# The depthwise convolution of one sample moved from TensorE's products to taps on VectorE, inside the attention of the sample before it

## The chip, the cores and the metric

The kernel runs on one core of one Trainium2 chip. The metric is the time of one execution on the device, in microseconds (us). It covers the whole program: sixteen samples, from the first load to the last store.

## The reference, cut to what matters

```python
x = x + L0(gn(x))      # whitening: power iterations on a covariance over all samples, once
x = x + L1(gn(x))      # deformable convolution, depthwise 3x3 in front of it
x = x + L2(gn(x))      # window attention: 64 windows of 49 tokens + 1, 16 heads of 32
x = x + L3(gn(x))      # masked 3x3 convolution, 128 -> 128 channels

# in L1; x is [16, 128, 56, 56], f32 throughout
xproj = x @ in_w + in_b
x1 = depthwise_conv3x3(x, dw_w) + dw_b          # one 3x3 filter for each channel
mu, var = x1.mean(-1), ((x1 - mu) ** 2).mean(-1)   # over the 128 channels of a pixel
x1 = gelu((x1 - mu) / sqrt(var + 1e-5) * ln_g + ln_b)
offset, mask = x1 @ off_w + off_b, softmax(x1 @ mask_w + mask_b)
out = bilinear_samples(xproj, offset, mask) @ out_w + out_b
```

## The kernel before, in words

Channels lie on the 128 partitions, and a sample is 3136 pixels on the free axis, in seven chunks of 8 rows (448 pixels). Every engine's program is written out by hand in its own order, and semaphores are all that ties them together. After a start that works out the whitening (some 490 us) one loop runs over the samples. Its body has two stages.

The first stage, `windows(i, n)`, is the attention of sample i. It runs in 32 **slots** (`for s in range(PAIRS)`), each for two windows and all heads. Between the attention's operations each slot carries a piece of the next sample's (n = i + 1) L1. The second stage, `sample_tiles(n, i)`, does the sampling of n and the rest of i, in 35 steps.

In slot s the attention's operations are, engine by engine and in this order:
- TensorE: `scores(s + 1)` (L747), `turn_exps(s)` (transposes, L758), `weigh(s - 1)` (L774), `values(s + 1)` (L733), two `queries_keys` (L725; slots 0 to 26 only). Ahead of `turn_exps(s)` stands `taken(s - 1, n)`, a wait until the banks that the last slot's piece of L1 used have been read, and a wait until both `queries_keys` of the last slot have been copied out. Ahead of the `queries_keys` stands a wait for VectorE's `turned(s)`.
- VectorE: `shift(s + 1)`, a maximum (L1738) and a subtraction (L1740) on the scores; `turned(s)`, a copy of half the transposed numbers (L1747); `normalise(s - 1)` (L1754, L1756); a copy of the odd `queries_keys` (L1732).
- ScalarE: a copy of the other half (L1140), the exponentials (L1134), copies of values and of the even `queries_keys` (L1127, L1122).

The piece of L1 has a fixed place in a slot: `before_first` at the slot's head and `before_last` at its end on VectorE and ScalarE, and `before5` and `before4` (named after the PSUM bank) behind the `queries_keys` on TensorE. Which piece a slot carries is set by constants, `GN0_AT, XP_AT, DW_AT, VAR_AT, BC_AT, OFF_AT = 2, 4, 8, 16, 18, 24`:
- slots 4 to 7 hold the projection of the image, two chunks a slot: ScalarE writes tiles (L1091), TensorE projects them (L671), and VectorE adds the bias into `img` one slot later (L1697);
- slots 8 to 14 hold the depthwise convolution, one chunk a slot, as nine products (L663) of the padded input `vp` with `dwc`, nine 128 x 128 matrices that hold the filter's diagonal times the centring matrix (identity minus 1/128), so that the sum comes out less its mean over the channels. ScalarE reads each chunk twice in the slot after it (L1071 to `x1c`, L1072 its square to `y1`);
- slot 16 holds the variance (L713); in slot 17 VectorE takes the reciprocal of seven rows of standard deviations (L1718);
- slots 18 to 21 spread these rows over the channels (L677), and VectorE multiplies them in (L1705);
- at the end of slot 22 ScalarE does the Gelu; slots 24 and 25 hold the projection to offsets and mask; slots 27 and 28 hold the mask's sum and product, and slots 29 to 31 the three `by_row` (L1640, L1646) for the sampling's first chunk.

`Chain.step` on VectorE and ScalarE makes the engine wait until the operation just issued is done. SyncE's queue issues `windows_out(i, s)` (L444) in each slot. In slot 9 it also issues `image_columns` (16 copies, L401 and L403), and in slot 11 `image_rows` (L408, L409).

For sample 0 the same pieces of L1 run ahead of the loop with no attention between them. The last sample's attention (the 16th block) carries no next sample.

Of the kernel before, what the change touches and what calls it, by code (L numbers as in the profile page):

```python
# [45 lines left out]
POW_D, POW_P = 9, 9  # L46
DVE_A, DVE_COV, DVE_POW = 20, 12, 22
ACT_MAIN = 14
DVE_PRE, DVE_MAIN, DVE_BLK, DVE_END = 6, 112, 69, 46

GN0_AT, XP_AT, DW_AT, VAR_AT, BC_AT, OFF_AT = 2, 4, 8, 16, 18, 24
TWO = (CHUNKS + 1) // 2
# [46 lines left out]
def build(nc, a):  # L99
    with ExitStack() as ctx:  # L100
# [13 lines left out]
        dwc = sb("dwc", [C, P9, C])  # L114
# [77 lines left out]
        mask16, mean128, centre = cv(C), cv(C), cv(C)  # L192
# [106 lines left out]
        cp_col, cp_img = sig("columns_copied", 2 * TY * 16), sig("rows_copied", 2 * 16)  # L299
        dw_p, dw_s = sig("dw_psum", CHUNKS), sig("dw_sbuf", CHUNKS)  # L300
# [38 lines left out]
        block = ctx.enter_context(nc.Block())  # L339
        WEIGHTS = 18 * 16  # L340
# [213 lines left out]
        def _(pe):  # L554
# [82 lines left out]
            def taken(s, n):  # L637
# [5 lines left out]
                elif DW_AT <= s < DW_AT + CHUNKS:  # L643
                    pe.wait_ge(dw_s.sem, dw_s.at(n, s - DW_AT + 1))
# [41 lines left out]

            def before4(s, n):

                if XP_AT <= s < XP_AT + TWO:
                    project_in(n, 2 * (s - XP_AT) + 1, 4)  # L690
                elif BC_AT <= s < BC_AT + TWO:
                    spread_rows(n, 2 * (s - BC_AT) + 1, 4)
                else:
                    project_bias(0, 4)
                    project_tile(n, 0, 2 * (s - OFF_AT), 4).then_inc(of_p.sem, 1)

            def before5(s, n):
# [6 lines left out]
                elif DW_AT <= s < DW_AT + CHUNKS:  # L704
# [311 lines left out]
            for s in range(PAIRS):  # L1016
                if in_bank5(s):
                    taken(s - 1, 0)
# [15 lines left out]
        def _(act):  # L1034
# [29 lines left out]
            def before_first(s, n):  # L1064
# [18 lines left out]
            def before_last(s, n):  # L1083

                if XP_AT - 1 <= s < XP_AT - 1 + TWO:
                    if s == XP_AT - 1:
                        act.wait_ge(gn_ab[0].sem, gn_ab[0].at(n))
                    for k in range(2 * (s - (XP_AT - 1)), min(2 * (s - (XP_AT - 1)) + 2, TR)):
# [4 lines left out]
                elif XP_AT - 1 + TWO <= s < XP_AT - 1 + 2 * TWO:  # L1093
                    for k in range(2 * (s - (XP_AT - 1 + TWO)), min(2 * (s - (XP_AT - 1 + TWO)) + 2, CHUNKS)):
                        rows = slice(k * ROWS, (k + 1) * ROWS)
                        nc.scalar.activation(vp_in[:, rows, :], xa[:, k * CH:(k + 1) * CH].rearrange("c (h w) -> c h w", w=W),
# [895 lines left out]
```

## Time and profile before

| | us |
|---|---|
| time, median of 3 runs | 11480.75 (11474.91 to 11494.1) |
| time of the profiled execution | 11494.43 |
| its span, first to last instruction | 11492.6 |
| TensorE matmul busy | 9424.9 (82%) |
| TensorE weight load busy | 5065.9 (44%) |
| VectorE busy | 6877.1 (60%) |
| ScalarE busy | 3657.9 (32%) |

The mean granted clock of TensorE was 0.869 of full speed. The busy shares are means over stages that differ, so the rows below are read stage by stage. **M(s)** stands for the start of VectorE's maximum (L1738) number s of a stage, s from 0 to 31. M(s) to M(s + 1) is one slot's length, with TensorE's piece of L1 from slot s - 1 in it. The stage looked at starts with M(0) at 5689.93 us. In it M(4) = 5716.14, M(9) = 5753.10, M(16) = 5844.29, M(17) = 5850.52, M(19) = 5870.58, M(23) = 5909.55 and M(31) = 5979.59, and the second stage's first `multiply` starts at 5993.97.

### The profile page before, as it was taken

The page shows a single profiled execution, that of the slowest core. Times are in us where ns is not written, and L with a number is a line of the kernel's source. Part 1 is how long each engine was busy: PE and PEld are TensorE (multiplying, and loading weights), DVE is VectorE, ACT ScalarE, POOL GpSimd, SP SyncE. Part 2 cuts the span into 40 slices and gives each one's busy share as a digit, 9 for nine tenths or more (in the row PEclk, how much of TensorE's full clock was granted, in tenths as well). Part 3 has the DMA queues.
Part 4 walks back from the last instruction along what each step waited for, and adds up shares of the span by engine and source line. Part 5 has one row for each costly group of instructions (what it writes and reads, how often), then busy time and mean ns, then how long its engine had stood idle before and what let it go on. Part 6 is the DMA issues. An engine that isn't in the chain of part 4 may idle for free.

```text
span 11492.6 us, 291312 instructions
## 1 busy us (share of the span) xinstructions
PE 9424.9 (82%) x125822; PEld 5065.9 (44%) x125822; DVE 6877.1 (60%) x8513; ACT 3657.9 (32%) x5874; POOL 216.2 (2%) x254
## 2 busy tenths in 40 slices
PE   5578888897888889798888878888797888888887
PEld 5324444353444435344443534435354443534444
DVE  2365756647466564846657475665747566574663
ACT  0023333242333324333232433324233332423322
POOL 0000000000000000000000000000000000000000
PEclk7668898898989888898888989889898988989888
DMA  4001101111110111111011111101011011111101
GB/s 99 17 0 33 41 25 36 30 33 35 36 42 19 39 33 31 37 35 40 22 39 29 36 38 33 35 26 41 27 37 39 26 35 30 35 34 36 41 17 51
DMA packets 230329, 391.97 MB, mean 34 GB/s; under 512 B 25200, under 2 KB 166480, under 8 KB 221776
## 3 DMA queue, kind: packets, MB, share of 16 engines
q1 hardware_dynamic: 229008, 372.66, 11.7%
q8 instruction: 1036, 16.97, 0.6%
q14 instruction: 285, 2.33, 0.1%
HBM read 192.47 MB, written 130.55 MB: 28 GB/s over the span
## 4 chain that ended last, share of the span: by engine, by line
PE 62%; DVE 20%; issue 10%; ACT 6%; DMA 1%; POOL 0%; DVEq 0%; SPq 0%; ACTq 0%; POOLq 0%
PE ps L663 13%; PE ps L857 9%; PE ps L725 8%; PE ps L733 4%; DVE arena L1663 4%; PE ps L758 4%; PE ps L774 4%; DVE arena L1640 3%; PE ps L956 3%; DVE arena L1646 3%; PE ps L946 3%; PE ps L747 2%; PE ps L685 2%; DVE arena L1629 1%; PE ps L682 1%
## 5 line engine op out<-in xcount | busy, mean ns | idle before, releaser
L857 PE MATMUL ps<-arena,ident 64*64 64x512 f32 x5600 | 1972.1, 738 | 923.4 <-DVE arena L1663 890.2
L859 PE MATMUL ps<-arena,ident 48*64 48x512 f32 x5600 | 1978.9, 740 | 0.0
L1663 DVE TENSOR_TENSOR arena<-arena 112x2560 f32<-112x2560 f32 x560 | 1573.5, 2817 | 2.4 <-PE ps L859 2.4
L857 PEld LDWEIGHTS ps<-arena,ident 64*64 64x64 f32 x5600 | 529.7, 158 | 2051.8 <-issue 2041.4
L1738 DVE TENSOR_REDUCE arena<-ps 128x16 f32<-128x800 f32 x512 | 505.8, 988 | 929.0 <-PE ps L747 921.2
L725 PE MATMUL ps<-arena,wqk 128*128 128x400 f32 x2048 | 964.9, 595 | 101.9 <-DVE arena L1747 54.4
L1732 DVE COPY arena<-ps 128x400 f32<-128x400 f32 x512 | 294.6, 575 | 1119.0 <-PE ps L725 1119.0
L663 PE MATMUL ps<-vp,convw 128*128 128x448 f32 x2016 | 819.5, 552 | 23.6 <-ACT vp L1269 23.6
L758 PE MATMUL ps<-ident,arena 128*128 128x128 f32 x4096 | 621.1, 300 | 213.2 <-ACT arena L1072 66.7
L663 PE MATMUL ps<-vp,dwc 128*128 128x448 f32 x2016 | 786.6, 543 | 8.3 <-ACT arena L1072 7.5
L1646 DVE TENSOR_TENSOR arena<-arena 112x576 f32<-112x576 f32 x1008 | 764.0, 758 | 34.9
L774 PE MATMUL ps<-arena 64*64 64x33 f32 x32768 | 681.8, 235 | 92.1 <-issue 53.1
L733 PE MATMUL ps<-wv,arena 128*64 128x256 f32 x4096 | 636.7, 437 | 103.2 <-ACT arena L1140 92.5
L774 PEld LDWEIGHTS ps<-arena 64*64 64x64 f32 x32768 | 613.7, 151 | 198.2 <-issue 198.0
L1640 DVE TENSOR_TENSOR arena<-arena 112x1728 f32<-112x1728 f32 x336 | 656.0, 1953 | 3.4
L725 PEld LDWEIGHTS ps<-arena,wqk 128*128 128x128 f32 x2048 | 355.5, 210 | 608.9 <-issue 238.1
L758 PEld LDWEIGHTS ps<-ident,arena 128*128 128x128 f32 x4096 | 492.5, 153 | 261.1 <-issue 126.4
L1134 ACT ACTIVATE arena<-arena 128x800 f32<-128x800 f32 x512 | 447.8, 875 | 446.1 <-DVE arena L1740 445.1
L663 PEld LDWEIGHTS ps<-vp,convw 128*128 128x128 f32 x2016 | 371.2, 192 | 480.1 <-issue 456.4
L747 PEld LDWEIGHTS ps<-arena 32*64 32x64 f32 x32768 | 403.6, 134 | 366.8 <-issue 358.3
L663 PEld LDWEIGHTS ps<-vp,dwc 128*128 128x128 f32 x2016 | 371.8, 189 | 397.2 <-issue 335.1
L1140 ACT ACTIVATE arena<-ps 128x512 f32<-128x512 f32 x512 | 305.7, 597 | 742.2 <-PE ps L758 742.1
(285 smaller groups left out, 12500.5 us busy)
## 6 DMA issues: line engine op xcount, KB each, us to landing
windows_out<-arena SPq DMA_DIRECT2D x1024, 100.0 KB
arena<-windows_out SPq DMA_DIRECT2D x224, 256.0 KB, 3.9
arena<-windows_out SPq DMA_DIRECT2D x224, 192.0 KB, 3.4
arena<-in_wqk SPq DMA_DIRECT2D x16, 2048.0 KB, 8.8
arena<-in_x_t SPq DMA_DIRECT2D x16, 1568.0 KB, 11.5
arena<-in_x SPq DMA_DIRECT2D x16, 1568.0 KB, 6.7
arena<-arena SPq DMA_DIRECT2D x32, 784.0 KB
out_x<-xb SPq DMA_DIRECT2D x112, 224.0 KB, 1.9
```

The lines of the kernel that those rows point to most:

```text
L663: mm = nc.tensor.matmul(ps[:, bank, 0:CH], weights[:, tap, :], vp[:, ROWS * k + dy:ROWS * k + dy + ROWS, dx:dx + W], start=(tap == 0), sto ...
L725: nc.tensor.matmul(ps[:, 5 - m % 2, 0:NWY * NTOK], wqk[:, m * C:(m + 1) * C], xwb[b % 2][:, :, 0:NTOK], start=True, stop=True).then_inc(qk ...
L733: mm = nc.tensor.matmul(ps[hh * SLOT:(hh + 1) * SLOT, 4, wi * 256:(wi + 1) * 256], xwb[b % 2][:, 2 * pr + wi, :], wv[:, hh * 256:(hh + 1) ...
L747: mm = nc.tensor.matmul(ps[wi * SLOT:(wi + 1) * SLOT, r, place * NTOK:(place + 1) * NTOK], qk[b % 2][32 * r:32 * r + 32, m, w:w + SLOT], q ...
L758: mm = nc.tensor.transpose(ps[:, 4 + q, k * C:(k + 1) * C], e_sb[u][:, 8 * q + 2 * k:8 * q + 2 * k + 2, :], ident)
L774: mm = nc.tensor.matmul(ps[wi * SLOT:(wi + 1) * SLOT, 6 + hh, (kk * 4 + r) * VD:(kk * 4 + r + 1) * VD], et[u][hh * SLOT:(hh + 1) * SLOT, a ...
L857: nc.tensor.matmul(ps[half, 3, :], ident[0:SLOT, 0:SLOT], prod[0:SLOT, ring(c, dy), dx, :], start=(s < 2), stop=(s >= TAPS - 2), skip_grou ...
L859: mm = nc.tensor.matmul(ps[half, 4, :], ident[SLOT:PT, SLOT:], prod[SLOT:PT, ring(c, dy), dx, :], start=(s < 2), stop=(s >= TAPS - 2), ski ...
L1640: ownm.step(V.tensor_tensor(tt[0:PT, :].rearrange("p (a n) -> p a n", a=3), hat[0:PT, :, 0, :], hat[0:PT, bb, 1:2, :].to_broadcast([PT, 3, ...
L1646: ins = V.tensor_tensor(k5, k5, tt[0:PT, aa * HN:(aa + 1) * HN].rearrange("p (x y n) -> p x y n", x=3, y=3), ALU.add)
L1663: V.tensor_tensor(prod[0:PT, ring(c, dy), :, :].rearrange("p k (n e) -> p k n e", e=CG), taps.to_broadcast([PT, SHIFTS, N64, CG]), for_tap ...
L1738: ownb.step(V.tensor_reduce(mxs[u].rearrange("p (r m) -> p r m", r=4), sv, AX.X, ALU.max))
```

## The change

The nine products with `dwc` go. VectorE now sums the nine taps itself: `depthwise(n, j)` multiplies a shifted view of `vp` by one filter value for each channel and adds it to `x1c`, two chunks (896 pixels) at once, 36 operations a sample (four blocks of nine; the last block has one chunk, 448 pixels). Three of them stand in each of the slots 5 to 16: behind `shift`, behind `turned`, and behind the copy of the `queries_keys`. TensorE then does the centring alone, one product of `centre` with each chunk (slots 12, 13, 15 and 17, up to two a slot in banks 5 and 4), which ScalarE reads as before. The other pieces move in the table: the padded input is written first (slots 3 to 6), the image's projection goes to slots 8 to 11, the variance from slot 16 to 18, the spreading from 18 to 20 and the offsets from 24 to 25. The third `by_row` of the first chunk moves from slot 31 into the second stage, behind its first `multiply`. `image_columns` and `image_rows` follow the projection, from slots 9 and 11 to 13 and 15. In the lines below, `pe` is TensorE, `dve` VectorE, `act` ScalarE.

```diff
+GN0_AT, V1_AT, XP_AT, VAR_AT, BC_AT, OFF_AT = 2, 3, 8, 18, 20, 25
+DW_BLOCKS = (CHUNKS + 1) // 2
+DW_SLOTS = (5, 5, 5) + (6, 6, 6) + (7, 7, 7) + (8, 8, 8) + (9, 9, 9) + (10, 10, 10) + (11, 11, 11) + (12, 12, 12) + (13, 13, 13) + (14, 14, 14) + (15, 15, 15) + (16, 16, 16)
+CT_AT = {12: (0, 1), 13: (2, 3), 15: (4, 5), 17: (6,)}
-GN0_AT, XP_AT, DW_AT, VAR_AT, BC_AT, OFF_AT = 2, 4, 8, 16, 18, 24
...
+            def centred(n, k, bank):
+                pe.wait_ge(dw_d.sem, dw_d.at(n, k // 2 + 1))
+                nc.tensor.matmul(ps[:, bank, 0:CH], centre, x1c[:, k * CH:(k + 1) * CH], start=True, stop=True
+                                 ).then_inc(dw_p.sem, 1)
...
-                elif DW_AT <= s < DW_AT + CHUNKS:
-                    k = s - DW_AT
-                    pe.wait_ge(v1_in.sem, v1_in.at(n, min(k + 2, CHUNKS)))
-                    for dy in range(3):
-                        mm = conv_row(k, 5, dwc, dy)
-                    mm.then_inc(dw_p.sem, 1)
+                elif s in CT_AT:
+                    centred(n, CT_AT[s][0], 5)
...
+            def depthwise(n, j):
+
+                b, tap = j // P9, j % P9
+                ks = dw_block(b)
+                dy, dx = tap // 3, tap % 3
+                acc = x1c[:, ks[0] * CH:(ks[-1] + 1) * CH].rearrange("c (h w) -> c h w", w=W)
+                around = vp[:, ROWS * ks[0] + dy:ROWS * (ks[-1] + 1) + dy, dx:dx + W]
+                if tap == 0:
+                    dve.wait_ge(v1_in.sem, v1_in.at(n, min(ks[-1] + 2, CHUNKS)))
+                    ownp.step(V.tensor_scalar(acc, around, dww[:, tap:tap + 1], None, ALU.mult))
+                    return
+                ins = V.scalar_tensor_tensor(acc, around, dww[:, tap:tap + 1], acc, ALU.mult, ALU.add)
+                if tap == P9 - 1:
+                    ins.then_inc(dw_d.sem, 1)
+                else:
+                    ownp.step(ins)
...
-                elif OFF_AT + 5 <= s < OFF_AT + 8:
+                elif OFF_AT + 5 <= s < OFF_AT + 7:
                     by_row(n, 0, s - (OFF_AT + 5))
...
-                        if c and dy == 0:
+                        if dy == 0:
                             by_row(n, c, 2)
```

VectorE in the loop's first stage, before, one slot of the depthwise stretch:

```order
L1738 TENSOR_REDUCE arena<-ps 128x16
L96 REGISTER_ALU
L1740 TENSOR_TENSOR arena<-ps,arena 128x800
L1747 COPY arena<-ps 128x512
L1754 RECIPROCAL arena<-ps 128x16
L96 REGISTER_ALU
L1756 TENSOR_TENSOR arena<-ps,arena 128x512
L1729 REGISTER_ALU
L1732 COPY arena<-ps 128x400
```

The same engine now, slot 10 (L1739 is a tap, L1713 the image's bias that was L1697, L105 the wait of `Chain.step`):

```order
L1776 TENSOR_REDUCE arena<-ps 128x16
L105 REGISTER_ALU
L1778 TENSOR_TENSOR arena<-ps,arena 128x800
L1739 SCALAR_TENSOR_TENSOR arena<-vp,cols,arena 128x896
L105 REGISTER_ALU
L1785 COPY arena<-ps 128x512
L1739 SCALAR_TENSOR_TENSOR arena<-vp,cols,arena 128x896
L1792 RECIPROCAL arena<-ps 128x16
L1794 TENSOR_TENSOR arena<-ps,arena 128x512
L1770 COPY arena<-ps 128x400
L1739 SCALAR_TENSOR_TENSOR arena<-vp,cols,arena 128x896
L1713 TENSOR_TENSOR arena<-ps,inb_row 112x512 x2
```

Three taps have come in between the six operations, and in slots 9 to 12 two bias additions stand with them.

TensorE before, from one slot's depthwise products to the next slot's:

```order
L663 MATMUL ps<-vp,dwc 128x448 x9
L747 MATMUL ps<-arena 64x50 x32
L758 MATMUL ps<-ident,arena 128x128 x8
L774 MATMUL ps<-arena 64x33 x32
L733 MATMUL ps<-wv,arena 64x256 x4
L725 MATMUL ps<-arena,wqk 128x400 x2
```

TensorE now, slot 12 to slot 13 (L704 is the centring; L765, L776, L792, L751 and L743 are the five attention groups):

```order
L704 MATMUL ps<-arena,centre 128x448 x2
L765 MATMUL ps<-arena 64x50 x32
L776 MATMUL ps<-ident,arena 128x128 x8
L792 MATMUL ps<-arena 64x33 x32
L751 MATMUL ps<-wv,arena 64x256 x4
L743 MATMUL ps<-arena,wqk 128x400 x2
```

Nine products a slot in seven slots have become two, two, two and one product in four slots.

## Rows read from the trace of the kernel before

**Rows 1.** The page: the chain that ended last, by engine.

```profile
PE 62%; DVE 20%; issue 10%; ACT 6%; DMA 1%; POOL 0%; DVEq 0%; SPq 0%; ACTq 0%; POOLq 0%
```

**Rows 2.** Stretches: length; PE, PEld, DVE, ACT, POOL busy (x); granted clock; DMA.

```profile
5716.14:5753.10 36.96, 34.62 (x796) 24.89 (x796) 25.12 (x40) 24.25 (x34) 0.00 (x0) 1.00 0.10 31
5753.10:5844.29 91.19, 87.23 (x1162) 49.31 (x1162) 28.66 (x43) 30.72 (x51) 0.00 (x0) 1.00 0.22 52
5850.52:5870.58 20.06, 19.22 (x388) 10.79 (x390) 10.80 (x13) 8.72 (x12) 0.00 (x0) 1.00 0.08 23
5870.58:5909.55 38.97, 36.68 (x532) 21.50 (x528) 20.67 (x33) 10.42 (x17) 0.00 (x0) 0.69 0.08 23
5909.55:5979.59 70.04, 55.86 (x1264) 36.40 (x1266) 40.60 (x57) 37.20 (x55) 2.87 (x2) 0.90 0.09 26
...
11120.16:11125.72 5.56, 5.56 (x149) 3.72 (x150) 4.01 (x6) 2.58 (x4) 0.00 (x0) 1.00 0.13 39
5880.15:5890.90 10.75, 10.72 (x152) 6.56 (x152) 5.35 (x8) 2.58 (x4) 0.00 (x0) 0.64 0.07 21
5971.84:5979.59 7.75, 6.61 (x215) 5.24 (x215) 7.49 (x10) 2.33 (x4) 1.43 (x1) 0.92 0.12 35
```

**Rows 3.** TensorE in time order, one slot with depthwise products: start, length, line.

```profile
5769.39 1.71 PE L725 MATMUL ps<-arena,wqk 128*128 128x400 f32 x4
5770.94 7.02 PE L663 MATMUL ps<-vp,dwc 128*128 128x448 f32 x18
5777.89 0.89 PE L747 MATMUL ps<-arena 32*64 32x50 f32 x64
```

**Rows 4.** VectorE in time order, the same slot; in brackets idle time and releaser.

```profile
5765.72 0.99 DVE L1738 TENSOR_REDUCE arena<-ps 128x16 f32<-128x800 f32 x1 [7.10 <-PE ps L747]
5766.75 0.99 DVE L1740 TENSOR_TENSOR arena<-ps,arena 128x800 f32<-128x800 f32 x1
5767.66 0.68 DVE L1747 COPY arena<-ps 128x512 f32<-128x512 f32 x1
5768.52 0.26 DVE L1754 RECIPROCAL arena<-ps 128x16 f32<-128x16 f32 x1 [0.18 <-PE ps L774]
5768.90 0.69 DVE L1756 TENSOR_TENSOR arena<-ps,arena 128x512 f32<-128x512 f32 x1
5771.14 0.57 DVE L1732 COPY arena<-ps 128x400 f32<-128x400 f32 x1 [1.55 <-PE ps L725]
5778.82 0.99 DVE L1738 TENSOR_REDUCE arena<-ps 128x16 f32<-128x800 f32 x1 [7.11 <-PE ps L747]
```

**Rows 5.** VectorE by line and shape: count, busy us, mean ns, idle before.

```profile
L1697 DVE TENSOR_TENSOR arena<-ps,inb_row 112x512 f32<-112x512 f32 x112 | 77.5, 692 | 39.9 <-PE ps L671 39.9
L1882 DVE SCALAR_TENSOR_TENSOR xb<-ps,cols,xb 128x448 f32<-128x448 f32 x112 | 76.5, 683 | 621.6 <-PE ps L663 621.6
L1877 DVE SCALAR_TENSOR_TENSOR arena<-arena,cols,vp 128x3136 f32<-128x3136 f32 x16 | 55.7, 3480 | 0.0
L1420 DVE TENSOR_SCALAR arena<-arena 128x256 f32<-128x256 f32 x16 | 5.7, 355 | 0.6
```

**Rows 6.** TensorE in time order at the lower clock, inside 5880.15:5890.90.

```profile
5885.71 2.65 PE L725 MATMUL ps<-arena,wqk 128*128 128x400 f32 x4
```

**Rows 7.** SyncE's queue: `image_columns`, first and last of 16 issues.

```profile
5783.42 0.99 SPq L401 DMA_DIRECT2D arena<-arena  x1
...
5797.25 0.83 SPq L403 DMA_DIRECT2D arena<-arena  x1
```

**Rows 8.** VectorE in time order, the second stage's head.

```profile
5993.97 2.82 DVE L1663 TENSOR_TENSOR arena<-arena 112x2560 f32<-112x2560 f32 x1
5999.17 0.46 DVE L1606 TENSOR_REDUCE softmax_max<-ps 112x32 f32<-112x288 f32 x1 [2.38 <-PE ps L685]
```

**Rows 9.** Two source lines: min/median/max ns, first and last start.

```profile
L663 PE MATMUL ps<-vp,dwc x2016: 537/538/643, 526.6 to 10583.9; 128*128 128x448 f32 x184
L713 PE MATMUL ps<-arena,varsel x224: 539/539/543, 584.6 to 10601.0; 128*7 128x448 f32 x112
```

More of the change, by code:

```diff
@@ L339, in build, with dw_block @@
         block = ctx.enter_context(nc.Block())
+        def dw_block(b):
+            return range(2 * b, min(2 * b + 2, CHUNKS))
         WEIGHTS = 18 * 16
@@ L690, in before4 @@
                     project_in(n, 2 * (s - XP_AT) + 1, 4)
+                elif s in CT_AT:
+                    centred(n, CT_AT[s][1], 4)
                 elif BC_AT <= s < BC_AT + TWO:
@@ L1016, in _ @@
             for s in range(PAIRS):
+                taken(s - 1, 0)
                 if in_bank5(s):
[L1018 removed]
                     before5(s, 0)
@@ L1083, in before_last @@
             def before_last(s, n):
-                if XP_AT - 1 <= s < XP_AT - 1 + TWO:
-                    if s == XP_AT - 1:
+                if V1_AT <= s < V1_AT + TWO:
+                    if s == V1_AT:
                         act.wait_ge(gn_ab[0].sem, gn_ab[0].at(n))
+                    for k in range(2 * (s - V1_AT), min(2 * (s - V1_AT) + 2, CHUNKS)):
+                        rows = slice(k * ROWS, (k + 1) * ROWS)
+                        nc.scalar.activation(vp_in[:, rows, :], xa[:, k * CH:(k + 1) * CH].rearrange("c (h w) -> c h w", w=W),
+                                             ACT.Identity, bias=sm[:, 9:10], scale=sm[:, 8:9]).then_inc(v1_in.sem, 1)
+                elif XP_AT - 1 <= s < XP_AT - 1 + TWO:
                     for k in range(2 * (s - (XP_AT - 1)), min(2 * (s - (XP_AT - 1)) + 2, TR)):
@@ L1092, in before_last @@
                                              bias=sm[:, 9:10], scale=sm[:, 8:9]).then_inc(v_t.sem, 1)
[L1093 to L1096, printed above, removed]
-                                             ACT.Identity, bias=sm[:, 9:10], scale=sm[:, 8:9]).then_inc(v1_in.sem, 1)
                 elif OFF_AT < s <= OFF_AT + 2:
@@ L1349, in _ @@
             own.step(V.tensor_tensor(centre, ident, mean128, ALU.subtract))
-            for tap in range(P9):
-                V.tensor_scalar(dwc[:, tap, :], centre, dww[:, tap:tap + 1], None, ALU.mult)
             V.tensor_tensor(stack[:, :], ident[:, 0:SLOT], ident[:, SLOT:], ALU.add)
@@ L1710, in before_first, with depthwise_of @@
                     shift_mask(n, 0, s - 1 - OFF_AT)
+            def depthwise(n, j):
[13 more added lines that the diff above has]
+                    ownp.step(ins)
+            def depthwise_of(s, n, place):
+                for j in range(dw_first(s) + place, dw_first(s + 1), 3):
+                    depthwise(n, j)
             def before_last(s, n):
@@ L1926, in _ @@
                 before_first(s, 0)
+                for place in range(3):
+                    depthwise_of(s, 0, place)
                 before_last(s, 0)
```

38 lines of the change are left out of this document (24 added, 14 removed).

## The prediction, made before the changed kernel ran

> **What bounds the kernel now.** I read the chain that ended last first. TensorE holds 62% of it and VectorE 20% [rows 1], so work taken off TensorE should count where it is the one waited for, and work put on VectorE may count too. The cut into stretches shows where [rows 2]. The seven slots with depthwise products, M(9) to M(16), take 91.19 us, 13.0 each. TensorE is busy for 87.23 of them, at full granted clock, and VectorE for 28.66. A slot with no piece of L1 takes 5.56 us at full clock. The order in time inside one depthwise slot gives the reason: the nine products take 7.02 us [rows 3], and VectorE idles 7.10 us before its maximum, released by the scores that stand behind these products on TensorE [rows 4]. So in these seven slots the products lie bare on the path, some 50 us a sample, and VectorE has 7 us of room a slot.
>
> At the stage's end it is the other way round. The slot 5971.84 to 5979.59 holds one `by_row` and takes 7.75 us, of which VectorE is busy 7.49 [rows 2]. There VectorE is the bound.
>
> **The cost of a tap.** The trace has no multiply-add of 896 elements. It has one of 448 at 683 ns and one of 3136 at 3480 ns [rows 5], which is 1.04 ns an element between them, so 683 + 448 x 1.04 = 1.15 us. The second reads a shifted view of `vp` as the taps do, so the view costs nothing extra. From below, the same slope from nought gives 0.93; from above 1.25, for the wait behind each tap that lets nothing overlap. I take 1.15, the value between the two rows. The four first taps are single-source: 256 elements take 355 ns [rows 5], so 896 take between 0.36 and the multiply-add's 1.15; I count 0.7. A tap of 448 is 0.68.
>
> The Trainium skill (VectorE: DVE Perf Modes, the perf-mode tier table) says that a float32 `tensor_scalar` in SBUF yields two elements a cycle and a two-tensor operation one. By that, an estimate, 640 more elements than in the 355 ns row cost 0.33 us and the first tap 0.69. The slope of 1.04 ns agrees with the one-a-cycle half; no row here shows the other for long operands.
>
> **A slot with taps (5 to 13).** VectorE's own six operations are 0.99 + 0.99 + 0.68 + 0.26 + 0.69 + 0.57 = 4.2 us [rows 4], and three taps are 3.45: 7.6 us in a row. Does TensorE keep up? Its `queries_keys` wait for the copy L1747, which now ends 0.99 + 0.99 + 1.15 + 0.68 = 3.8 us after the maximum's start. They take 1.71 [rows 3] and end at 5.7 with 0.2 for the hand-over, while VectorE is at a tap and `normalise` until 5.9. The scores (0.89, [rows 3]) run under the copy and the third tap. TensorE's 5.56 us of work fits, and VectorE alone sets the slot: 7.6 us at full clock.
>
> **The sum, slot by slot, for the sample in the rows.**
> - M(4) to M(9): 36.96 us with the image's projection in it [rows 2]. Now two slots without work for TensorE (6.6 and 6.0, a little over the bare 5.56 since ScalarE also writes `vp`) and three with taps, 22.8: 35.4. Saved 1.5.
> - M(9) to M(19): 91.19 + 6.23 + 20.06 = 117.5 us [rows 2]; the 6.23 is M(16) to M(17). Now it is M(9) to M(21). Four slots have taps and two bias additions of 0.69 [rows 5], 7.6 + 1.3 = 8.9 each: 35.6. Two slots follow with two centring products. A product is 7.02 / 9 = 0.78 us; the second waits for the last copy, and behind it stand the scores: 5.9 + 0.57 + 0.78 + 0.89 + 0.2 = 8.3 each, 16.6. ScalarE's four reads of them hide under VectorE's maximum, subtraction and first tap. The last block's taps are 0.47 shorter each, so a slot of them is 6.2 us by VectorE's row; the ring through TensorE is longer there, since ScalarE's reads of the centred chunks hold up the transposes: 7.1, 8.0 with centring, 7.1, and 7.0 for slot 17: 29.2. Variance and reciprocal stay as they are, 20.1. Together 101.5. Saved 16.0.
> - The spreading, 38.97 us, only moves.
> - M(23) to M(31): 70.04 us in eight slots; now M(25) to M(31), six slots. Two things go. The slot that lay between the Gelu and the offsets' products disappears, 6 us (between the bare 5.56 and 6.6, at the stretch's clock of 0.90); the stall for ScalarE's Gelu and the first products now fall in one slot. And the third `by_row` goes with its slot, 7.75 [rows 2]. Saved 13.8.
> - Second stage: that `by_row` costs 7.75 - 3.6 = 4.15 us (3.6 is VectorE's work in a slot without `queries_keys`). It stands behind the first `multiply`, where VectorE idles 2.38 us [rows 8]. Lost 1.8.
>
> The sum is 1.5 + 16.0 + 13.8 - 1.8 = 29.5 us a sample, in 15 rounds 442 us. Ahead of the loop, sample 0's convolution lies bare from 526.6 to 584.6 us [rows 9]. In its place stand 24 taps of 1.15, 8 of 0.68 and 4 first ones, 36 us, with 5 us of bias additions; they start some 10 us sooner, since `vp` is now written first. I count 20 us. The last attention block is untouched. 11494.4 - 462 = 11032 for the profiled execution. It ran 13.7 us above the median of the runs, so 11018 on their scale; I say **11020**.
>
> **What I cost at nothing.** SyncE's 16 copies occupy its queue for 14.7 us [rows 7], now in slots of 8 us instead of 13. `windows_out(14)` queues behind them, and the `normalise` that needs its landing comes two slots later, some 20 us on; half that distance would stall VectorE by a few us a sample. `image_columns` waits for bias additions that end in slot 12, one slot ahead. ScalarE's tile writing fits in its idle time (30.72 us busy of 91.19, [rows 2]).
>
> **The rivals.**
> 1. *TensorE's clock falls.* In the depthwise stretch the granted clock is 1.00, at the 2.4 GHz level, and TensorE hardly rests. In the spreading it is 0.69: it fell behind a slot in which TensorE waited for the long reciprocal, and mostly ran at 1.2 GHz, with `queries_keys` at 2.65 us for 1.71 [rows 3, 6], and a slot at 10.75 us and clock 0.64 [rows 2]. Slots with taps leave TensorE idle for 2 us of 7.6, so its clock may fall there. A slot at the lower level costs between 8.6 (the ring with 1 us more in `queries_keys`) and 10.75; I take 9.8, or 2.2 more. If half of the twelve tap slots are so, 13 us a sample go, 200 us in all: 11220. If only a few are, 11080. For it: the bare slots of the last block already show TensorE full at 5.56. Against it: those near the bare 5.56, with waits inside, stay at 1.00, and the projection and centring fill the gap in six of the twelve. Chance 0.22 for a loss of 70 to 250 us.
>
>  The Trainium skill (TensorE: Matmul & The Clock Gate, the section on oscillation in real kernels) says that idle gaps in TensorE drop it to half clock and that dense products release it. It speaks against this change, which trades the densest stretch for gaps. The trace agrees on two levels and on full clock in the dense stretch.
>
> 2. *The clock falls in all of slots 5 to 26.* This is the slower side. Twelve slots lose 2.2 us (26), variance and offsets another 8, and what is behind the reciprocal stays low: 34 us lost against 29.5 gained, 15 x 4.5 = 68 us, less the 20 of sample 0: 11530. It decides once tap slots average 10 us. Chance 0.04.
> 3. *VectorE's row is longer than its sum.* Each tap waits for its own end and stands between two operations that TensorE or ScalarE wait for. If each slot takes 8.6 instead of 7.6, 12 us a sample go: 180 us, 11200. Against it: the `by_row` slot, with four such waits, takes 7.75 us at 7.49 busy. Chance 0.12 for 70 to 200 us lost.
> 4. *More is won*: the low end of the tap's price, 0.93, makes a slot 7.0 us, so twelve slots give 8 us a sample, 120 us in all: 10900. For it speaks nothing but that no row shows the operation at this length. Chance 0.06.
> 5. *The taps hide nothing*: the slots stay at 13 us since something else waits. Idle 7.10 on VectorE, released by scores, excludes it. Chance 0.01 for within 0.2%.
>
> **How the numbers follow.** My forecast, 10960 to 11090, has 0.55. Rivals 1 and 3 have 0.34 together, two thirds of it below 11220; rival 4 has 0.06, rivals 2 and 5 have 0.05. A range from 10920 (half of rival 4's gain) to 11220 leaves out some 0.16 to 0.2. Its upper end also covers taps at 1.25 us, 0.3 a slot or 54 us in all. A measurement of this kernel tells some 0.2%, 23 us. Faster 0.94, same 0.01, slower 0.05.
>
> **What the changed profile would show.** Right: M(9) to M(13) at 8.9 us a slot, VectorE without idle time between them, the multiply-adds of 896 at 1.15 us, PE busy down by some 650 us, VectorE's up by 36 x 16 taps, some 570 us, and clock 1.00 in slots 5 to 16. Wrong: clock under 0.8 there, idle time before L1770 with the `queries_keys` as releaser, or `normalise` waiting for a DMA in slots 16 and 17.

## The result, and the profile after

The changed kernel takes 11085.18 us (median of five runs, 11059.27 to 11137.82) where the kernel before takes 11482.89 (median of five, 11474.91 to 11494.1). The ratio is 0.9657, with a 95% interval of 0.9633 to 0.9682. The forecast was 11020, with a range of 10920 to 11220: faster, as said, and 65 us short of the gain.

The profiled execution of the changed kernel took 11137.82 us, the slowest of its five, at a mean granted clock of 0.848. Lengths of slots below are means over the 15 rounds of the loop, from the starts of VectorE's maximum (now L1776), unless a row is shown.

The page's chain, by engine, against [rows 1]:

```profile
PE 55%; DVE 25%; issue 12%; ACT 6%; DMA 1%; DVEq 0%; SPq 0%; POOL 0%; ACTq 0%; POOLq 0%
```

TensorE's share of the chain falls by 7 points and VectorE's rises by 5. Matmul busy time falls from 9424.9 to 8908.2 us, 517 and not the 650 of the forecast: the sampling's products, which the change leaves as they are, took 72 us longer (L875 2043.6, and 1972.1 before). VectorE's rises from 6877.1 to 7395.0.

The cut into stretches, of the same round as in [rows 2] and with the same columns. The stage now starts with M(0) = 5512.86; the rows are M(4) to M(9), M(9) to M(19), M(19) to M(21), M(21) to M(25), M(25) to M(31):

```profile
5538.16:5572.57 34.41, 29.49 (x748) 20.12 (x748) 29.57 (x41) 21.55 (x34) 0.00 (x0) 1.00 0.11 30
5572.57:5650.23 77.66, 69.06 (x1545) 45.47 (x1543) 68.45 (x95) 40.41 (x64) 0.00 (x0) 1.00 0.25 58
5650.23:5677.67 27.44, 22.53 (x388) 12.08 (x390) 10.89 (x13) 9.87 (x15) 0.00 (x0) 0.88 0.18 53
5677.67:5716.50 38.83, 36.45 (x532) 20.75 (x528) 20.61 (x32) 10.40 (x17) 0.00 (x0) 0.69 0.08 23
5716.50:5775.60 59.10, 47.62 (x953) 30.17 (x956) 28.63 (x42) 31.07 (x45) 2.87 (x2) 0.77 0.08 22
```

The seven slots with depthwise products are gone. The ten slots M(9) to M(19) take 77.66 us, and VectorE is busy for 68.45 of them. The granted clock stays at 1.00, the 2.4 GHz level, in every slot with taps. The third row is the surprise: variance and reciprocal were costed unchanged, at 20.1 us, and take 27.44.

VectorE in time order, one slot with three multiply-adds, against [rows 4]:

```profile
5557.57 0.99 DVE L1776 TENSOR_REDUCE arena<-ps 128x16 f32<-128x800 f32 x1
5558.60 0.99 DVE L1778 TENSOR_TENSOR arena<-ps,arena 128x800 f32<-128x800 f32 x1
5559.50 1.14 DVE L1739 SCALAR_TENSOR_TENSOR arena<-vp,cols,arena 128x896 f32<-128x896 f32 x1
5560.68 0.69 DVE L1785 COPY arena<-ps 128x512 f32<-128x512 f32 x1
5561.29 1.14 DVE L1739 SCALAR_TENSOR_TENSOR arena<-vp,cols,arena 128x896 f32<-128x896 f32 x1
5562.46 0.26 DVE L1792 RECIPROCAL arena<-ps 128x16 f32<-128x16 f32 x1
5562.75 0.69 DVE L1794 TENSOR_TENSOR arena<-ps,arena 128x512 f32<-128x512 f32 x1
5563.36 0.56 DVE L1770 COPY arena<-ps 128x400 f32<-128x400 f32 x1
5563.84 1.14 DVE L1739 SCALAR_TENSOR_TENSOR arena<-vp,cols,arena 128x896 f32<-128x896 f32 x1
5565.11 0.99 DVE L1776 TENSOR_REDUCE arena<-ps 128x16 f32<-128x800 f32 x1
```

No row carries a bracket: in this slot VectorE never idles, where it idled 7.10 us before. The slot is 7.54 us. VectorE by line and shape, columns as in [rows 5]:

```profile
L1739 DVE SCALAR_TENSOR_TENSOR arena<-vp,cols,arena 128x896 f32<-128x896 f32 x384 | 438.8, 1143 | 0.7
L1739 DVE SCALAR_TENSOR_TENSOR arena<-vp,cols,arena 128x448 f32<-128x448 f32 x128 | 86.5, 676 | 0.3
L1737 DVE TENSOR_SCALAR arena<-vp,cols 128x896 f32<-128x896 f32 x48 | 32.5, 678 | 2.1 <-ACT vp L1108 2.1
```

**Two new losses.** The first is in M(19) to M(20). That slot holds the variance; its like took 10.92 us before and takes 17.33 now. TensorE in time order:

```profile
5651.82 1.11 PE L792 MATMUL ps<-arena 64*64 64x33 f32 x58
5656.41 0.43 PE L792 MATMUL ps<-arena 64*64 64x33 f32 x6 [3.48 <-issue]
5656.77 1.97 PE L751 MATMUL ps<-wv,arena 128*64 128x256 f32 x8
5658.68 3.04 PE L743 MATMUL ps<-arena,wqk 128*128 128x400 f32 x4
5661.64 6.03 PE L731 MATMUL ps<-arena,varsel 128*7 128x448 f32 x14
```

In the midst of the 64 products of `weigh` (L792) TensorE stands still for 3.48 us with nothing to wait for: "issue". Then it runs at the lower level for a while, `queries_keys` at 3.04 us for 1.71. The granted clock, which was 1.00 up to the pause, is 0.50 behind it:

```profile
5656.40:5660.00 3.60, 3.59 (x16) 1.90 (x17) 0.95 (x2) 0.60 (x1) 0.00 (x0) 0.50 0.19 57
```

The pause is there in 15 of 15 rounds, 3.4 us in the mean; of before, no round has one in its variance slot. Ahead of it SyncE issues the two copies of `image_rows`, the second (L423) 0.9 us behind the first:

```profile
5645.65 0.87 SPq L422 DMA_DIRECT2D arena<-arena  x1
```

The DMA view shows what is moved at that time, first for 5645.5 to 5654.0 and then, the row of the instruction queue alone, for 5654 to 5656 (queue: packets, MB, share of 16 engines):

```profile
q1 hardware_dynamic: 394, 1.89, 74.5%
```

```profile
q8 instruction: 1, 0.02, 2.7%
```

For 8.5 us no packet with instructions comes. Then one of 16 KB comes at 5654.1, and 2.3 us later TensorE goes on. By the single records the copies' 196 packets of 8 KB run from M(19) - 3.1 to M(19) + 4.1 in this round, and the instruction packet starts at M(19) + 3.9. Over the 15 rounds this packet starts at M(19) + 3.3 to + 4.3, and TensorE goes on 2.2 to 2.5 us later.

The second loss is at the head of the second stage. Steps 0 and 1, from one `multiply` to the next, took 6.06 and 5.94 us and take 7.96 and 9.79. VectorE there in time order, and SyncE's queue:

```profile
5789.97 2.81 DVE L1679 TENSOR_TENSOR arena<-arena 112x2560 f32<-112x2560 f32 x1
5792.70 1.95 DVE L1656 TENSOR_TENSOR arena<-arena 112x1728 f32<-112x1728 f32 x1
5794.69 2.35 DVE L1662 TENSOR_TENSOR arena<-arena 112x576 f32<-112x576 f32 x3
5797.07 0.46 DVE L1622 TENSOR_REDUCE softmax_max<-ps 112x32 f32<-112x288 f32 x1
...
5805.78 0.42 DVE L1846 TENSOR_REDUCE t8s<-arena 128x8 f32<-128x256 f32 x1 [5.03 <-DMA arena<-windows_out]
```

```profile
5797.06 0.37 SPq L463 DMA_DIRECT2D arena<-in_wqk  x1
5797.62 1.28 SPq L469 DMA_DIRECT2D arena<-windows_out  x2
```

The same three operations in the kernel before:

```profile
6003.98 0.42 DVE L1802 TENSOR_REDUCE t8s<-arena 128x8 f32<-128x256 f32 x1 [1.13 <-DMA arena<-windows_out]
```

```profile
5994.86 0.37 SPq L449 DMA_DIRECT2D arena<-in_wqk  x1
5996.53 1.25 SPq L455 DMA_DIRECT2D arena<-windows_out  x2
```

The `by_row` (L1656, L1662) pushes the softmax's maximum from 5.20 to 7.10 us behind the first `multiply`: the 1.9 us of the forecast. But SyncE waits for this `by_row` before it loads the attention's weights (L463), and the load of the first tokens (L469) is queued behind. It is issued 7.65 us after the first `multiply` and was 2.56 ([rows 8] has that `multiply`'s start), and VectorE waits 5.03 us for it instead of 1.13.

### The profile page after: what moved, and what is told of

The parts are those of the page before. It is cut to its first block, busy times and chain, and to the rows that moved or that the text cites. A ratio compares the mean times of both kernels' runs of the same rounds, so it can differ in the third digit from the quotient of the medians.

```text
span 11135.9 us, 288961 instructions
## 1 busy us (share of the span) xinstructions
PE 8908.2 (80%) x124030; PEld 4802.9 (43%) x124030; DVE 7395.0 (66%) x9080; ACT 3642.6 (33%) x5874; POOL 199.6 (2%) x254
## 3 DMA queue, kind: packets, MB, share of 16 engines
q8 instruction: 1020, 16.71, 0.6%
q14 instruction: 286, 2.34, 0.1%
## 4 chain that ended last, share of the span: by engine, by line
PE 55%; DVE 25%; issue 12%; ACT 6%; DMA 1%; DVEq 0%; SPq 0%; POOL 0%; ACTq 0%; POOLq 0%
PE ps L875 10%; PE ps L743 7%; PE ps L678 7%; DVE arena L1679 4%; PE ps L776 4%; PE ps L751 4%; PE ps L792 3%; DVE arena L1656 3%; DVE arena L1662 3%; PE ps L974 3%; DVE arena L1739 3%; PE ps L964 3%; PE ps L765 2%; PE ps L700 2%; DVE arena L1645 1%
## 5 line engine op out<-in xcount | busy, mean ns | idle before, releaser
L875 PE MATMUL ps<-arena,ident 64*64 64x512 f32 x5600 | 2043.6, 763 | 965.9 <-DVE arena L1679 930.8
L877 PE MATMUL ps<-arena,ident 48*64 48x512 f32 x5600 | 2050.5, 764 | 0.0
L875 PEld LDWEIGHTS ps<-arena,ident 64*64 64x64 f32 x5600 | 546.4, 163 | 2146.3 <-issue 2135.7
L743 PE MATMUL ps<-arena,wqk 128*128 128x400 f32 x2048 | 975.7, 602 | 175.1 <-DVE arena L1785 127.9
L1662 DVE TENSOR_TENSOR arena<-arena 112x576 f32<-112x576 f32 x1008 | 764.0, 758 | 34.9
L776 PE MATMUL ps<-ident,arena 128*128 128x128 f32 x4096 | 620.3, 300 | 206.7 <-ACT arena L1215 57.4
L792 PE MATMUL ps<-arena 64*64 64x33 f32 x32768 | 674.6, 235 | 106.9 <-issue 69.9
L751 PE MATMUL ps<-wv,arena 128*64 128x256 f32 x4096 | 657.7, 447 | 107.3 <-ACT arena L1158 95.5
L792 PEld LDWEIGHTS ps<-arena 64*64 64x64 f32 x32768 | 610.3, 151 | 209.2 <-issue 209.0
L1776 DVE TENSOR_REDUCE arena<-ps 128x16 f32<-128x800 f32 x512 | 505.0, 986 | 250.5 <-PE ps L765 245.1
L743 PEld LDWEIGHTS ps<-arena,wqk 128*128 128x128 f32 x2048 | 374.5, 215 | 679.3 <-issue 220.6
L1656 DVE TENSOR_TENSOR arena<-arena 112x1728 f32<-112x1728 f32 x336 | 656.1, 1953 | 3.4
L776 PEld LDWEIGHTS ps<-ident,arena 128*128 128x128 f32 x4096 | 491.1, 153 | 254.5 <-issue 138.1
L765 PEld LDWEIGHTS ps<-arena 32*64 32x64 f32 x32768 | 405.5, 136 | 374.4 <-issue 366.4
L765 PE MATMUL ps<-arena 32*64 32x50 f32 x32768 | 469.1, 234 | 95.7 <-DVE arena L1778 38.3
L1739 DVE SCALAR_TENSOR_TENSOR arena<-vp,cols,arena 128x896 f32<-128x896 f32 (+1 forms) x512 | 525.4, 1026 | 1.0
```

Source lines behind the costliest of these rows:

```text
L743: nc.tensor.matmul(ps[:, 5 - m % 2, 0:NWY * NTOK], wqk[:, m * C:(m + 1) * C], xwb[b % 2][:, :, 0:NTOK], start=True, stop=True).then_inc(qk ...
L751: mm = nc.tensor.matmul(ps[hh * SLOT:(hh + 1) * SLOT, 4, wi * 256:(wi + 1) * 256], xwb[b % 2][:, 2 * pr + wi, :], wv[:, hh * 256:(hh + 1) ...
L765: mm = nc.tensor.matmul(ps[wi * SLOT:(wi + 1) * SLOT, r, place * NTOK:(place + 1) * NTOK], qk[b % 2][32 * r:32 * r + 32, m, w:w + SLOT], q ...
L776: mm = nc.tensor.transpose(ps[:, 4 + q, k * C:(k + 1) * C], e_sb[u][:, 8 * q + 2 * k:8 * q + 2 * k + 2, :], ident)
L792: mm = nc.tensor.matmul(ps[wi * SLOT:(wi + 1) * SLOT, 6 + hh, (kk * 4 + r) * VD:(kk * 4 + r + 1) * VD], et[u][hh * SLOT:(hh + 1) * SLOT, a ...
L875: nc.tensor.matmul(ps[half, 3, :], ident[0:SLOT, 0:SLOT], prod[0:SLOT, ring(c, dy), dx, :], start=(s < 2), stop=(s >= TAPS - 2), skip_grou ...
```

## The experiments

Edits are against the changed kernel unless said otherwise.

**1. `image_rows` issued later.** Slot 24, 18 or 16 instead of 15.

```diff
-                        if s == XP_AT + TWO + 3:
+                        if s == 24:
                             image_rows(n)
```

> The changed kernel, with image_rows issued in slot 24 instead of slot 15. In the changed kernel M(18) to M(19) takes 17.3 us in the mean of 15 rounds, where 10.9 were expected; in it TensorE stands still for 3.4 us in the middle of weigh, waiting for nothing that the profile names, some 5 us after the two large copies of image_rows were issued, and its clock falls behind that. Theory A, the copies hold up the loading of TensorE's instructions: the slot goes back to 11 us, 95 us are saved in all (about 0.86% of the time), and the copies fall beside the Gelu's stall, where TensorE waits anyway. Theory B, the pause belongs to that place of the program or to the centring in the slot before: the slot stays at 17 us and the time is unchanged.

> The changed kernel, with image_rows issued in slot 18 instead of slot 15. Theory A (the copies hold up the loading of TensorE's instructions): the pause of about 3.4 us leaves M(18) to M(19) and turns up some 5 us behind the copies' new place, in M(21) to M(23), so that it moves with them and little of the time is saved. Theory B (the pause belongs to the place): M(18) to M(19) stays at 17 us.

> The changed kernel with image_rows issued one slot later (16 for 15), where its copies begin about at M(19). In the changed kernel an instruction packet of 16 KB that lands near M(19) - 0.4 us without the copies lands at M(19) + 3.9 us with them, and TensorE stands still for 3.4 us. Theory A (the copies hold up any instruction packet that falls among them): the packet near M(19) comes in time, the next one (near M(19) + 5.7) is late, and the pause moves behind M(20) or shrinks. Theory B (only the place M(19) to M(20) in the program is sensitive): the pause stays there. Theory C (TensorE's clock or VectorE's long reciprocal makes slot 19 long): 17 us stay whatever the copies do; image_rows in slots 18 and 24 already speak against it.

(The expectations call the slot M(19) to M(20) of this text M(18) to M(19).)

Slot 24 took 10994.56 us (10989.9 to 10999.94, four runs; ratio 0.9579, 0.9563 to 0.9595), 91 under the changed kernel. M(19) to M(20) is 11.59 us, 5.7 less, which is 86 us in 15 rounds, and no round has the pause. TensorE in that slot:

```profile
5560.32 1.14 PE L792 MATMUL ps<-arena 64*64 64x33 f32 x64
5561.38 1.08 PE L751 MATMUL ps<-wv,arena 128*64 128x256 f32 x8
5562.40 1.71 PE L743 MATMUL ps<-arena,wqk 128*128 128x400 f32 x4
5564.03 5.43 PE L731 MATMUL ps<-arena,varsel 128*7 128x448 f32 x14
```

Its DMA view for the stretch that answers to the 8.5 us above, 5554.0 to 5562.5:

```profile
q1 hardware_dynamic: 336, 0.56, 20.9%
q8 instruction: 2, 0.03, 1.3%
```

Two instruction packets come where none did, one of them at M(19) - 0.4. Beside the pause the changed kernel loses time here by the lower level: against these rows its `values` (L751), `queries_keys` (L743) and variance (L731) took 2.8 us more.

Slot 18 took 11000.43 us (10992.76 to 11012.26; ratio 0.9586, 0.957 to 0.9602), nearly the same. Its copies run from 5.9 to 13.1 us after M(20). An instruction packet that comes 7.7 us after M(20) without copies comes at 9.1 there, 1.4 late, and TensorE has no pause "issue" in that stretch. This packet starts in the midst of the copies, 3.8 to 4.3 us before their end in each round: they delay it, and don't hold it to their end. That the pause would move along with the copies did not come true.

Slot 16 took 10993.05 us in one run, M(19) to M(20) 11.70. There the copies run from M(19) - 0.3 to + 7.0 or a little more. The packet near M(19) comes just ahead of them, in time. The next starts at their end: in all 15 rounds within 1.2 us of it, in eight within 0.3. The window from 5588.2 to 5595.5 and, its instruction queue alone, the one from there to 5597 (M(19) = 5588.56):

```profile
q1 hardware_dynamic: 263, 1.67, 81.7%
```

```profile
q8 instruction: 1, 0.02, 3.7%
```

So the copies hold an instruction packet back in both kernels, and it costs nothing in this one: TensorE then has its 14 long products and waits for the reciprocal. The kernel before issued `image_rows` at another place, and none of its instruction packets fell among the copies: over 15 rounds the nearest came 0.5 us before them and 1.0 behind their end.

Two things speak for it that the held packet is TensorE's own. Its queue brings one packet for 243 of TensorE's matmuls and weight loads in either kernel (251644 and 1036 packets before, 248060 and 1020 now), while VectorE's instructions become more. And TensorE goes on 2.2 to 2.5 us behind the packet's start in each of the 15 rounds. The copies aren't the only way to such a pause. In M(8) to M(9) of the changed kernel 9 of 15 rounds have one of some 1.1 us, again ended 2.4 to 2.7 us behind a packet's start, and no packet of 8 KB or more but instructions is moved within 6 us of it. Ones of 0.9 to 1.0 us in the mean stand, in most rounds, in M(24) to M(25) and M(30) to M(31) of the kernel before.

**2. The third `by_row` back in slot 31.**

```diff
                 elif OFF_AT + 5 <= s < OFF_AT + 7:
                     by_row(n, 0, s - (OFF_AT + 5))
+                    if s == PAIRS - 1:
+                        by_row(n, 0, 2)
...
-                        if dy == 0:
+                        if c and dy == 0:
```

> The changed kernel, with the third by_row back in slot 31 behind the second one. Moving it was costed at 4.15 us saved in slot 31 and 1.8 lost at the head of the second stage; measured there are 5.8 us more in the second stage's first two steps. Theory A, the row of VectorE is full at both places and the by_row delays something else too: the first stage grows by 4.15 us, the second stage's head shrinks by 5.8, and the kernel gains 1.6 us a sample, 25 us. Theory B, the 5.8 us come from elsewhere (clock or other order): the head stays long and the kernel loses 4.15 us a sample, 60 us.

10990.0 us (10924.15 to 11061.17, four runs; ratio 0.9554, 0.9515 to 0.9593). The profiled execution is the slowest of the four. In it steps 0 and 1 are 6.06 and 6.06 us, 5.6 less, and the stage's end is 4.4 longer, so this edit by itself is worth 1.3 us a sample, 19 us. The median says 95, from four runs that lie 137 us apart. Of the two profiled executions this one is 77 us shorter, and most of the rest lies in parts that the edit doesn't touch. The slots M(21) to M(25), with the spreading, make 44 us: they take 34.7 us at a mean granted clock of 0.81, and 37.6 at 0.73 in the changed kernel. Step 7 of the second stage makes 37. It takes 14.5 to 18 us or, in some rounds, 24. TensorE at its start, in a round of either kind of the changed kernel:

```profile
5839.45 7.09 PE L909 MATMUL ps<-arena 128*128 128x64 f32 x32
...
6492.21 3.83 PE L909 MATMUL ps<-arena 128*128 128x64 f32 x32
```

The same 32 products run at half the clock in the first. The changed kernel has 5 such rounds of 15, this one 1, the kernel before none, and the kernels of the other experiments 0 to 5. What sets it is open.

**3. That part of the change alone, on the kernel before.** Its third `by_row` goes into the second stage.

```diff
-                elif OFF_AT + 5 <= s < OFF_AT + 8:
+                elif OFF_AT + 5 <= s < OFF_AT + 7:
                     by_row(n, 0, s - (OFF_AT + 5))
...
-                        if c and dy == 0:
+                        if dy == 0:
```

> One part of the change alone on the kernel before: the third by_row of the first chunk goes from slot 31 into the second stage behind its first multiply. The prediction's count: slot M(30) to M(31) 7.75 to 5.4, the stage's end (M(31) to the first multiply) 14.4 less 0 to 4.4, second stage plus 1.8; 15 x (-5) = -80 us. Theory A (SyncE's load of the attention weights waits for this by_row, and the load of the first tokens is queued behind it, so that VectorE waits for their landing): steps 0 and 1 of the second stage go from 6.06 + 5.94 to about 7.96 + 9.8, plus 5.8, against 2.4 saved in slot M(30) to M(31) and 0 to 4.4 at the stage's end: between -1.0 and +3.4 us a sample, -15 to +50 us in all.

11541.08 us (11504.96 to 11558.42, six runs) where before, on that chip, took 11483.94; ratio 1.0053, 1.0032 to 1.0074. Steps 0 and 1 are 7.96 and 9.78, as in the changed kernel. That is 5.7 us a sample more, and the stage's end is 1.9 shorter. The slot M(30) to M(31) stays at 7.74 us, where the count had 5.4. So the edit costs 3.8 us a sample, 57 us, and the medians differ by 57. The prediction's gain for it isn't there, and the loss is a little over the theory's upper end of 50. The profiled execution, the fastest of the six, hides it: its first stage is 3.3 us shorter, but 3.2 of them lie in M(19) to M(23), the spreading, which the edit doesn't touch and which ran at a granted clock of 0.80 for 0.71. VectorE's row with the wait:

```profile
6029.77 0.42 DVE L1802 TENSOR_REDUCE t8s<-arena 128x8 f32<-128x256 f32 x1 [4.98 <-DMA arena<-windows_out]
```

To load the tokens ahead of the weights would take the wait away without the `by_row`'s move, but the tokens land in memory that this `by_row` still reads, so no run here does that.

**4. All three taps at the slot's end.**

```diff
-                    if n is not None:
-                        depthwise_of(s, n, 0)
                     turned(i, s)
-                    if n is not None:
-                        depthwise_of(s, n, 1)
...
-                        depthwise_of(s, n, 2)
+                        for place in range(3):
+                            depthwise_of(s, n, place)
```

> The changed kernel, with all three taps of a slot behind the copy of the queries_keys instead of one at each of three places. Theory A, taps are cheap only where they stand in VectorE's wait for the queries_keys: that wait of 1.2 us, which the bare slot shows before L1770, comes back in each of the 12 slots and is added to the row, 12 x 1.2 x 15 = 216 us slower than the changed kernel. Theory B, only the sum of VectorE's work counts: no difference.

11335.32 us (11287.47 to 11372.91; ratio 0.986, 0.9825 to 0.9896). The same work costs 250 us more in another order, as theory A said with 216. The first stage is 17.0 us longer, M(6) to M(7) 8.83 for 7.17 and M(11) to M(12) 12.75 for 8.52. VectorE in its slot M(7) to M(8), and TensorE's `queries_keys` there:

```profile
5681.09 0.99 DVE L1776 TENSOR_REDUCE arena<-ps 128x16 f32<-128x800 f32 x1
...
5685.60 0.57 DVE L1770 COPY arena<-ps 128x400 f32<-128x400 f32 x1 [1.01 <-PE ps L743]
5686.10 3.51 DVE L1739 SCALAR_TENSOR_TENSOR arena<-vp,cols,arena 128x896 f32<-128x896 f32 x3
5683.76 1.81 PE L743 MATMUL ps<-arena,wqk 128*128 128x400 f32 x4 [1.63 <-DVE arena L1785]
```

VectorE now idles while TensorE computes `queries_keys`. Then it does three taps in a row, and TensorE, whose next `queries_keys` need a copy behind them, waits in its turn.

**5. One tap of the three left out.** The sum then lacks terms of the convolution: taps 1, 4, 7 of each block of nine (the second of a slot), taps 3 and 6 (the first), or taps 2 and 5 (the third). The edit in `depthwise`, here for the second:

```diff
+                if tap % 3 == 1:
+                    return
```

> The second of the three taps of each slot (the one between the copy of the transposed numbers and normalise) is left out, 12 of 36 taps a sample, so the convolution's sum lacks three of its nine terms; everything else stays. Theory A (VectorE's row sets the slots with taps): nine slots lose 1.14 us and three lose 0.68, 12.3 us a sample, 185 us in 15 rounds and 10 more for sample 0, so about 10890, and the slots without bias additions at 6.1 to 6.5. Theory B (the ring through TensorE sets them, since this tap lies beside TensorE's queries_keys): the slots stay within 0.3 us, 11030 or more.

> The first tap of a slot (behind the subtraction, ahead of the copy of the transposed numbers for which TensorE's queries_keys wait) is left out in two slots of three: taps 3 and 6 of each block of nine, 8 a sample, so the convolution's sum lacks two of its nine terms. In the run without the second tap the slots lost only 0.2 to 0.3 us where VectorE's row lost 1.14, and VectorE then stood idle ahead of its maximum, released by the scores. Theory A (two limits close together, VectorE's row at 7.5 us and the ring through TensorE at some 7.25, and this tap stands in both): the slots M(7) to M(9) and M(10) to M(12) lose about 1.0 to 1.1 us each, down to the 6.2 to 6.6 us of slots without taps; slots that begin a block stay. Theory B (TensorE's own row and its clock set the floor near 7.2): no more than 0.3 us is lost here too.

> The third tap of a slot (behind the copy of the odd queries_keys, last in VectorE's row) is left out in two slots of three: taps 2 and 5 of each block, 8 a sample. Theory A as for the run without the first tap: this tap stands in VectorE's row alone, so slots M(6) to M(8) and M(9) to M(11) lose 0.2 to 0.3 us as in the run without the second tap, and VectorE idles 0.8 us ahead of its maximum. Theory B (the row alone sets the slots, and the second tap's omission was hidden by something beside it): 1.1 us a slot.

Without the second: 11034.79 us (10997.93 to 11055.43; ratio 0.9594, 0.9566 to 0.9622). Without the first: 11038.9 (11006.66 to 11074.95; 0.9619, 0.9589 to 0.9649). Without the third: 11033.51, one run. Slots in us, taps left out in a slot marked with *:

| slot | all | no second | no first | no third |
|---|---|---|---|---|
| M(6) to M(7) | 7.17 | 6.92* | 7.18 | 5.99* |
| M(7) to M(8) | 7.54 | 7.26* | 6.35* | 7.37* |
| M(8) to M(9) | 7.57 | 7.64* | 7.53* | 7.75 |
| M(10) to M(11) | 8.74 | 8.37* | 8.03* | 8.49* |
| M(12) to M(13) | 7.68 | 7.43* | 7.67 | 6.97* |

A second tap is 1.14 us of VectorE's row and its omission gains 0.3. Without it VectorE idles ahead of the copy of the `queries_keys` (not ahead of the maximum, as the expectation for the first tap had it):

```profile
5527.37 0.57 DVE L1772 COPY arena<-ps 128x400 f32<-128x400 f32 x1 [0.81 <-PE ps L743]
```

So there is a ring of about 7.26 us: maximum, subtraction, first tap, copy, TensorE's `queries_keys`, their copy, third tap. It lies 0.3 us under VectorE's row. The first and the third tap are in both: where nothing else holds, each omission gains the full 1.2 (6.35 for 7.54, 5.99 for 7.17). For the third tap the expectation of 0.2 to 0.3 was wrong in M(6) to M(7), where 1.2 is gained, and in M(12) to M(13) with 0.7. It came true in M(7) to M(8) and M(10) to M(11). In M(7) to M(8) the scores close the ring in the third tap's place: they wait for the copy of the `queries_keys`, and the next maximum waits 1.02 us for them. TensorE's row of the run without the third tap:

```profile
5513.08 0.88 PE L765 MATMUL ps<-arena 32*64 32x50 f32 x64 [0.99 <-DVE arena L1772]
```

In M(8) to M(9) no omission gains anything, since there TensorE stops for 1.05 us in the midst of `weigh`, the pause without copies of experiment 1; the row of the run without the first tap:

```profile
5505.70 0.89 PE L792 MATMUL ps<-arena 64*64 64x33 f32 x45 [1.05 <-issue]
```

**6. Both repairs.** `image_rows` in slot 24 and the `by_row` in slot 31.

> Both repairs at once: image_rows issued in slot 24 and the third by_row of the first chunk back in slot 31. Theory A (two separate losses: the late instructions of TensorE behind image_rows, and what hangs on the by_row in the second stage) expects them to add. By the profiles of the single edits, slot M(19) to M(20) at 11.6 us, steps 0 and 1 of the second stage at 6.06 each, the stage's end 4.4 us longer: 15 x 1.5 = 22 us under the kernel with image_rows in slot 24 alone (10995), so about 10970. Theory B (the medians of the single edits, 91 and 95 us under the changed kernel, are both due to the edits in full) expects 10900. Theory C (both repaired the same loss) expects 10990 or more.

10954.95 us (10936.71 to 10969.81, five runs; ratio 0.9534, 0.9512 to 0.9556). That is 130 us under the changed kernel and 15 from the 10970 of the theory with two separate losses. M(19) to M(20) is 11.63 us, steps 0 and 1 are 6.06 and 6.00.

## Why the prediction was right, and where it was off

The direction, the place of the gain and the range were right. The sum by its terms, us a sample, for the profiled execution:

| term | forecast | measured |
|---|---|---|
| M(4) to M(9) | +1.5 | +2.7 |
| M(9) to M(19), taps and centring | 81.4 long | 77.7 long |
| M(19) to M(21), variance and reciprocal | 20.1 long | 26.5 long |
| both, against 117.5 | +16.0 | +13.4 |
| spreading | 0 | +0.7 |
| M(25) to M(31) | +13.8 | +14.9 |
| M(0) to M(4) | 0 | +0.2 |
| second stage | -1.8 | -8.7 |
| sum | 29.5 | 23.2 |
| ahead of the loop | +20 in all | +17 in all |

The measured column is a mean over 15 rounds on either side. The profiled execution gained 357 us of the 462: 15 x 23.2 + 17, less 8 in the last sample's part, whose cause is open. The executions without a profile do not tell where they gained their 398 in the median. How far the clock alone moves a term from one execution to the next can be seen in the spreading: it took 37.6 us at a granted clock of 0.73 here and 34.4 at 0.82 in the kernel with `image_rows` in slot 24.

- **The price of a tap** was right: 1.15 against 1.143 us, 0.68 against 0.676, the first tap 0.7 against 0.678. The Trainium skill's two elements a cycle for a one-source operation (VectorE: DVE Perf Modes, the perf-mode tier table) gave an estimate of 0.69 for it, and the trace agrees.
- **The slots with taps** were right in size, 7.6 against 7.54, and 8.9 against 7.7 to 8.7 with bias additions. These four slots took 33.1 us for 35.6: a sample has seven bias additions, and eight were counted (slot 12 has one), and in two of the slots one of the three taps is a first one, of 0.68 us, where the count had 1.15. "VectorE alone sets the slot" was only just right: the omissions show a second limit 0.3 us below, and that TensorE fits beside it holds only with the taps spread as they are (experiment 4).
- **Rival 1, the clock**: refuted, 1.00 in the slots with taps. The Trainium skill's warning of idle gaps (TensorE: Matmul & The Clock Gate, on oscillation in real kernels) did not bite there, with TensorE busy for 69.06 of 77.66 us. It did where TensorE had stood still, 3.48 us for want of instructions, and the granted clock was 0.50 behind it: the trace agrees. Rivals 2 and 3 fall with the same rows, rival 4 with the tap's 1.143, rival 5 with the result.
- **"Variance and reciprocal stay as they are"** failed: 6.4 us a sample, 96 in all. Under "what I cost at nothing" SyncE's copies were weighed for what is queued behind them on SyncE, and not for what they do to the delivery of instructions. Experiment 1 gives 91 us back. The 0.7 us a sample that stay have another cause: the transposes wait 0.63 us for ScalarE's reads of the last centred chunk (L1090), in the kernel of experiment 1 too, and nothing stood in their way before.
- **"Lost 1.8" for the `by_row`** failed: the price beside the softmax was right (1.9), but the step left out SyncE's queue, where two loads hang on this `by_row`. Steps 0 and 1 cost 5.8, so 4 us more, 60 in all. Experiment 3 shows it without the rest of the change: there the move costs 57 us where the prediction's count had a gain.
- The remainder of the second stage is step 7 at the lower clock (+2.3 us a sample in this execution) and step 16 (+1.1). They were not foreseen, and neither is explained.
- **M(25) to M(31)** looks better than it was. The forecast took 13.8 off the 70.04 us of the one round in the rows, so it had these six slots at 56.2, and they took 58.9. The gain of 14.9 is there because the mean of before was 73.8.

These misses, some 13 us a sample, were partly made up by terms that gained more than counted, some 7 us. That the time came out only 65 us above the forecast is so in part luck, while the price of a tap and the size of the slots with taps were understood.

## What to carry to other kernels

Where one engine's bare work covers another's idle time, moving it pays, and its price can be read from rows of other lengths of the same operation; but look for the ring through both engines, and spread the moved work so that each piece lies under what the other engine does. A moved step carries its waits along: ask each DMA queue what waits for it, and what stands behind that. And place bulk copies within SBUF where the busiest engine is in long instructions or in a wait.

## What the runs showed of the hardware that was not expected

Instructions come by DMA too, and bulk copies delay them. The page of the changed kernel has two queues for them: q8, by its count TensorE's, with 1020 packets and 16.71 MB, so 16 KB each, and q14 with 286 and 2.34 MB, so 8 KB each. With 196 packets of 8 KB in flight for 7.2 us, the packet due near M(19) - 0.4 us came at M(19) + 3.3 to + 4.3 in all 15 rounds, within 0.5 us of the copies' end, and TensorE stood still for 3.4 us and then ran at the lower level. The whole slot cost 5.7 us more. With the copies at another place (slot 18) a packet came 1.4 us late and cost no pause.

The Trainium skill (Runtime: NRT & Kernel Launch, on instruction fetch mechanics) says that each engine's instructions are refilled in 16 KiB blocks by a DMA queue of its own and that this is mostly hidden. The trace agrees on the size of the block for this queue and, in M(19) to M(20), not on "mostly hidden". It also says (DMA: Bandwidth & Descriptors, on queues and rings) that a DMA engine takes turns between queues only after a whole packet of typically 9 to 17 descriptors; by an estimate from the 196 packets, an engine's share of the two copies is 196 / 16, some 12 pieces, and of one copy 6. That would fit a refill that waits for the end of both copies, as with slots 15 and 16, or of one, as with slot 18, where it came 3.2 us after their start. No run here tests it by itself.
